# Products of the odd stages that leave out the border's block row

## The reference

```
def basic_block(x, w1, w2, stride=1, ds=None):
    out = relu(conv3(x, w1, stride) * BN_S)          # 3x3, padding 1
    out = conv3(out, w2, 1) * BN_S
    identity = conv1x1(x, ds, stride) * BN_S if ds is not None else x
    return relu(out + identity)

x = basic_block(x, e0b0c1, e0b0c2)                   # 64x64
x = basic_block(x, e0b1c1, e0b1c2)
f0 = x
x = basic_block(x, e1b0c1, e1b0c2, stride=2, ds=e1b0ds)   # 32x32
x = basic_block(x, e1b1c1, e1b1c2)
f1 = x
x = basic_block(x, e2b0c1, e2b0c2, stride=2, ds=e2b0ds)   # 16x16
x = basic_block(x, e2b1c1, e2b1c2)
x = (relu(deconv2(x, dec0w) * BN_S) + f1) * BN_S
x = (relu(deconv2(x, dec1w) * BN_S) + f0) * BN_S     # deconv2: 2x2 kernel, stride 2
```

## Time and profile before

| | |
|---|---|
| median of 3 runs | 89.10 us (89.04 to 89.35) |
| the profiled execution, its device time | 89.06 us |
| its span, first to last instruction | 87.3 us |
| TensorE busy with matmuls | 80.4 us, 92% of the span, 509 records |
| VectorE, ScalarE, GpSimd busy | 56.6, 43.8, 25.6 us |
| mean granted TensorE clock | 0.99 |

### The profile page before, as it was taken

How to read it: one execution, slowest core, us unless ns; L and a number is a source line. 1 busy time by engine, 2 the same in 40 slices (tenths; PEclk the granted TensorE clock), 3 DMA queues, 4 the chain that set the end, 5 groups by cost and what they waited for, 6 DMA issues and landing times.

```text
span 87.3 us, 1464 instructions
## 1 busy us (share of the span) xinstructions
PE 80.4 (92%) x509; PEld 72.0 (83%) x509; DVE 56.6 (65%) x166; ACT 43.8 (50%) x94; POOL 25.6 (29%) x39
## 2 busy tenths in 40 slices
PE   5999999999999999999999999999999999799700
PEld 3777999998778889999988777999999999587500
DVE  5569999799968696522223567999697877213450
ACT  6005214679555047455530239799999996001300
POOL 7200052799960000444452000100289100000330
PEclk9999999999999999999999999999999999999995
DMA  1979930023475106640000000000000000000075
GB/s 27 247 238 274 315 131 0 0 56 108 153 211 204 30 0 173 188 128 0 0 0 0 0 0 4 0 0 0 0 8 0 0 0 0 0 0 8 4 274 207
DMA packets 4183, 6.51 MB, mean 75 GB/s; under 512 B 464, under 2 KB 2128, under 8 KB 4176
## 3 DMA queue, kind: packets, MB, share of 16 engines
q1 hardware_dynamic: 4032, 6.29, 23.5%
q10 hardware_dynamic: 144, 0.13, 0.5%
HBM read 5.37 MB, written 1.05 MB: 74 GB/s over the span
## 4 chain that ended last, share of the span: by engine, by line
PE 91%; DVE 3%; issue 1%; DVEq 0%
PE psum L843 79%; PE psum L870 8%; DVE result L834 2%; PE psum L1023 1%; PE psum L886 1%; PE psum L863 1%; PE psum L1068 1%; PE psum L879 1%; DVE odd L756 0%; DVEq L175 0%; DVE last L754 0%; DVE flat L752 0%; DVE zeros L678 0%; DVEq L833 0%; DVE eps L680 0%
## 5 line engine op out<-in xcount | busy, mean ns | idle before, releaser
L498 POOL TENSOR_TENSOR odd<-relu,odd 128x363 fp32r<-128x363 f32 x12 | 13.6, 1150 | 15.4 <-ACT odd L563 15.4
L843 PE MATMUL psum<-shared,w_e0b0c 128*128 128x364 f32 x72 | 12.5, 331 | 0.0
L773 DVE SCALAR_TENSOR_TENSOR relu<-psum,inside 128x363 f32<-128x363 f32 (+1 forms) x16 | 8.1, 510 | 6.5 <-PE psum L843 5.1
L843 PEld LDWEIGHTS psum<-shared,w_e0b0c 128*128 128x128 f32 x72 | 12.0, 188 | 0.3 <-issue 0.3
L843 PE MATMUL psum<-shared,w_e0b1c 128*128 128x364 f32 x72 | 12.1, 328 | 0.0
L843 PEld LDWEIGHTS psum<-shared,w_e0b1c 128*128 128x128 f32 x72 | 12.0, 188 | 0.1
L843 PE MATMUL psum<-odd,w_e0b0c 128*128 128x512 f32 x48 | 11.6, 400 | 0.0
L843 PE MATMUL psum<-odd,w_e0b1c 128*128 128x512 f32 x48 | 11.6, 400 | 0.0
L843 PEld LDWEIGHTS psum<-odd,w_e0b1c 128*128 128x128 f32 x48 | 9.1, 189 | 2.2
L843 PEld LDWEIGHTS psum<-odd,w_e0b0c 128*128 128x128 f32 x48 | 9.1, 189 | 2.2
L563 ACT ACTIVATE odd<-relu 128x363 fp32r<-128x363 f32 x12 | 6.1, 507 | 7.2 <-DVE relu L773 7.2
(11 more groups left out here) (125 smaller groups left out, 126.2 us busy)
## 6 DMA issues: line engine op xcount, KB each, us to landing
x_sb<-x_in SPq DMA_DIRECT2D x4, 160.0 KB, 3.8
raw<-e0b0c_in SPq DMA_DIRECT2D x2, 256.0 KB, 4.8
raw<-e0b1c_in SPq DMA_DIRECT2D x2, 256.0 KB, 5.0
raw<-e1b1c_in SPq DMA_DIRECT2D x2, 256.0 KB, 3.2
raw<-e2b1c_in SPq DMA_DIRECT2D x2, 256.0 KB, 2.7
raw<-e1b0c_in SPq DMA_DIRECT2D x1, 448.0 KB, 3.7
raw<-e2b0c_in SPq DMA_DIRECT2D x1, 448.0 KB, 3.9
x_sb<-x_in SPq DMA_DIRECT2D x2, 192.0 KB, 4.0
```

The costliest lines, as they stand in the source:

```text
L498: pool.tensor_tensor(split_of(piece, 1), fp32_of(piece), split_of(piece, 0).bitcast(F32), ALU.subtract).then_inc(lo_ready, 1)
L773: last = dve.scalar_tensor_tensor(out=target, in0=sums, scalar=0.0, in1=mask, op0=ALU.max, op1=ALU.mult)
L843: last = pe.matmul(target, w, moving, start=(first and n == 0), stop=(final and n == len(terms) - 1), skip_group_check=skip)
```

## The change

Each product may now carry a pair of columns; the moving run and the PSUM target are then both cut to it. `inside_columns` gives the pair: a piece that holds the top row drops the first pitch - 1 columns where sy is below 1 (below 2 in a down stage), and a piece that holds the bottom row drops the last row (and the run's padding) where sy is 1 (2 in a down stage). The products that carry start or stop stay whole. In odd stages the order of the four shifts is turned (2, 3, 0, 1) where that lets start or stop fall on a whole product. Even stages, sides products, shortcuts and the decoder stay as they are.

```
             def products(target, terms, first=True, final=True, skip=False):
-                for n, (w, moving) in enumerate(terms):
-                    last = pe.matmul(target, w, moving, start=(first and n == 0),
-                                     stop=(final and n == len(terms) - 1), skip_group_check=skip)
+                for n, (w, moving, *columns) in enumerate(terms):
+                    ends = (first and n == 0) or (final and n == len(terms) - 1)
+                    columns = [] if ends else columns
+                    last = pe.matmul(within(target, columns), w, within(moving, columns), start=(first and n == 0),
+                                     stop=(final and n == len(terms) - 1), skip_group_check=skip or len(columns) > 0)
                 return last
+            def within(run, columns):
+                if not columns:
+                    return run
+                span = slice(*columns)
+                return run[:, span] if len(run.shape) == 2 else run[:, :, span]
+            def inside_columns(stage, sy, rows, above, below):
+                pitch = ODD_COLS[0] if stage.level == 0 else PITCH[stage.level]
+                whole = rows * pitch
+                if below and sy == (2 if stage.kind == "down" else 1):
+                    return [0, whole - pitch]
+                if above and sy < (2 if stage.kind == "down" else 1):
+                    return [pitch - 1, whole + 1]
+                return []
...
+                def columns(s):
+                    if stage.kind == "even":
+                        return []
+                    return inside_columns(stage, s // shifts, piece.rows, piece.row == 0,
+                                          piece.row + piece.rows == stage.total)
...
-                    whole = [[moving(half, shifts * sy + sx) for sy, sx in WHOLE] for half in range(2)]
+                    whole = [[(moving(half, shifts * sy + sx), *columns(shifts * sy + sx)) for sy, sx in WHOLE]
+                             for half in range(2)]
...
-                products(target, [(w[:, 0, s], moving(0, s)) for s in range(shifts ** 2)],
+                whole_first = [2, 3, 0, 1] if stage.kind == "odd" and piece.row == 0 else range(4)
+                products(target, [(w[:, 0, s], moving(0, s), *columns(s)) for s in whole_first],
                          first=not started, final=False)
                 wait_w_lo(pe, k)
-                products(target, [(w[:, 1, s], moving(0, s)) for s in range(shifts ** 2)], first=False, final=False)
-                low_terms = [(w[:, 0, s], moving(1, s)) for s in range(shifts ** 2)]
+                products(target, [(w[:, 1, s], moving(0, s), *columns(s)) for s in range(shifts ** 2)],
+                         first=False, final=False)
+                whole_last = [2, 3, 0, 1] if stage.kind == "odd" and piece.row > 0 else range(4)
+                low_terms = [(w[:, 0, s], moving(1, s), *columns(s)) for s in whole_last]
...
             def of_image(image, first):
                 for n in range(EARLY):
-                    pe.matmul(target[:, image], w[:, 0, n], whole[n][:, image], start=(first and n == 0),
-                              stop=False, skip_group_check=True)
+                    columns = [] if n == 0 else columns_2[n]
+                    pe.matmul(within(target[:, image], columns), w[:, 0, n], within(whole[n][:, image], columns),
+                              start=(first and n == 0), stop=False, skip_group_check=True)
...
-            products(target, [(w[:, 0, n], whole[n]) for n in range(EARLY, len(WHOLE))], first=False, final=False,
-                     skip=True)
+            products(target, [(w[:, 0, n], whole[n], *columns_2[n]) for n in range(EARLY, len(WHOLE))], first=False,
+                     final=False, skip=True)
...
-            products(target, [(w_sb[k][:, 0, s], shifted(flat2, s, RUN[2])) for s in range(4)]).then_inc(summed, 1)
+            products(target, [(w_sb[k][:, 0, s], shifted(flat2, s, RUN[2]),
+                               *inside_columns(STAGES[LEVEL2["e2b1c1"].stage], s // 2, ODD_ROWS[2], True, True))
+                              for s in range(4)]).then_inc(summed, 1)
```

More of the change, by code:

```diff
@@ L946, in moving @@
                     return source[:, half, images[0], first:first + run]
+                def columns(s):
[3 more added lines that the diff above has]
+                                          piece.row + piece.rows == stage.total)
                 pe.wait_ge(w_hi, k + 1)
                 if stage.kind == "down":
-                    whole = [[moving(half, shifts * sy + sx) for sy, sx in WHOLE] for half in range(2)]
+                    whole = [[(moving(half, shifts * sy + sx), *columns(shifts * sy + sx)) for sy, sx in WHOLE]
+                             for half in range(2)]
                     wait_source(piece, 0)
                     wait_w_lo(pe, k)
-                    products(target, [(w[:, part, n], m) for part in range(2) for n, m in enumerate(whole[0])],
+                    products(target, [(w[:, part, n], *m) for part in range(2) for n, m in enumerate(whole[0])],
                              final=False)
                     wait_source(piece, 1)
-                    products(target, [(w[:, 0, n], m) for n, m in enumerate(whole[1])], first=False, final=False)
+                    products(target, [(w[:, 0, n], *m) for n, m in enumerate(whole[1])], first=False, final=False)
                     pe.wait_ge(sides_by_act, images[-1] + 1)
@@ L1019, in _ @@
                      for sy, sx in WHOLE]
+            columns_2 = [inside_columns(STAGES[LEVEL2["e2b0c1"].stage], sy, ODD_ROWS[2], True, True) for sy, _ in WHOLE]
             def of_image(image, first):
                 for n in range(EARLY):
-                    pe.matmul(target[:, image], w[:, 0, n], whole[n][:, image], start=(first and n == 0),
-                              stop=False, skip_group_check=True)
+                    columns = [] if n == 0 else columns_2[n]
+                    pe.matmul(within(target[:, image], columns), w[:, 0, n], within(whole[n][:, image], columns),
+                              start=(first and n == 0), stop=False, skip_group_check=True)
             wait_half(pe, source_of_level(2, 0), 0)
```

## The result

The changed kernel takes 87.95 us (median of 4 runs, 87.89 to 88.33) against 89.07 (4 runs, 88.90 to 89.35): a ratio of 0.9889, interval 0.9869 to 0.9909. (The ratio on record isn't the quotient of the two medians, which is 0.9874.) Forecast were 88.1 from 89.10, a gain of 1.0; measured is 1.1. The profiled execution took 87.95 us, its span is 86.1 against 87.3.

What follows compares the result with a forecast made beforehand. TensorE bounds the kernel (92% busy, 91% of the last chain). Of 1.22 us in cut columns, 0.69 + 0.01 + 0.31 = 1.01 arrives: 89.06 - 1.01 = 88.05, forecast 88.1 with the median 0.04 higher; range 87.75 to 88.5.

Steps and rivals of the forecast that it cites:

- The price of a column: TensorE's wide matmuls at levels 0 and 1: 0.44 ns per column cut, from distances between starts, ends 0.43 and 0.48.
- Rival B: TensorE matmuls: columns worth a third, through the load or a cost of cutting the PSUM target; 88.8 us, chance 0.06.
- What is taken back: TensorE's waits behind the cuts: level 0 keeps 0.69 us, e1b0c1 0.01 of 0.21, the rest 0.31; sum 1.01.
- 0.01 of slack before the shortcut's load: Second image's shortcut in e1b0c2 waits for ScalarE's corner copies; only 0.01 us of e1b0c1's saving passes.
- Rival A: e1b0 waits on VectorE's and ScalarE's copies give way, so another 0.20 us arrives; 87.9 us, chance 0.15.
- GpSimd's low half: First image's last piece at level 0: ready for 13.78, TensorE coming at 13.81, just enough; 0.01 us charged.
- the second image's sides: e1b0c1: VectorE's copy plus 0.23 us gives 60.20 against a need at 60.24, so that half passes.
- the second down stage: Sides copies behind ScalarE's skip0 copies could start 0.18 us earlier; e1b1c1 asks for 0.15, so it fits.
- Rival C: First-stage low half, second image's sides and second down stage's sides each miss, costing 0.25 us; 88.35 us, chance 0.10.
- the 0.23 us from producer to matmul: At tight waits, a matmul needs its producer some 0.23 us before: 0.12 to the load, 0.11 more to the matmul.
- The cut of `of_image`: Level 2: cut from 82 to 74 columns costed at nothing, paced by 0.11 us loads; up to 0.03 us if wrong.
- Rival D: Tail from about 75 us: TensorE's clock falls to half, adding 3.3 us; 91.4 us, chance 0.03.

Runs made afterwards that it cites:

- e12: Changed kernel with the 48 cut products of level 0 over 260 columns, output not the reference's; single run, e0b1c1 10.85 us, 0.119 us a cut product.
- e8: Changed kernel with the 48 cut products of level 0 over 200 columns, output not the reference's; single run, e0b1c1 10.63 us, 0.110 us a cut product.
- e1: Changed kernel with the products of e1b0c1 whole again, all other cuts kept; 88.08 us, ratio 0.9875 to the kernel before.
- e6: Changed kernel with ScalarE's skip scaling moved ahead of its sides copies and VectorE's image 0 side copies each one place earlier; 87.58 us, ratio 0.9834.
- e7: Changed kernel with earlier ScalarE skip scaling and earlier VectorE image 0 side copies, but e1b0c1 whole again; 88.09 us, ratio 0.9879.
- e4: Changed kernel with ScalarE's scaling of image 0's skip moved into idle time before its first sides copies; 87.89 us, ratio 0.9867 to the kernel before.
- e5: Changed kernel with VectorE's side copies of image 0 each made one place earlier; 87.99 us, ratio 0.9861 to the kernel before.
- e2: Only the level 0 odd stages cut (48 matmuls, 1584 columns), against the kernel before; 88.42 us, ratio 0.9923.
- e9: The changed kernel once more, unaltered, on another chip; 87.98 us, ratio 0.9891 to the kernel before.

## Why the prediction was right

**The price of a column.** Taken from the shapes of the trace before as 0.44 ns; (11.98 - 11.64)/24/33 = 0.43 in e0b1c1, and e12 gives 0.45 over a hundred columns. Level 0 was forecast to shorten by 0.35 in each stage: 0.34 in e0b1c1 and 0.38 in e0b0c1. Rival B, columns worth less or a cut target that costs, is out by these and by e8 and e12.

**What is taken back.** This was the step that could have gone wrong by 0.20 us: all columns together would have been 1.22. That e1b0c1 brings 0.01 of its 0.21 was read from two small distances, 0.19 in place of 0.135 at the sides and 0.01 of slack before the shortcut's load. e1 shows it from one side, e6 against e7 from the other. Of the two waits the shortcut's is the one that binds: without it (e4) 0.08 arrive, without the other alone (e5) 0.01, without both 0.28. Rival A is out. The 0.01 of slack was right too: with ScalarE's list as it is the change, e1 and e5 all come to 9.49 or 9.50, with three different amounts of work or waiting ahead of the shortcut, and before the change it was 9.51.

**The tight places elsewhere.** GpSimd's low half, the second image's sides and the second down stage were worked out to pass with some hundredths, and all passed: no wait on GpSimd shows, and e1b1c1, e2b0c1 and e2b1c1 gave 0.14, 0.10 and 0.06 of the forecast 0.15, 0.10 and 0.06. Rival C is out. At the low half the margin is used up:

```profile
12.67 0.75 POOL L491 TENSOR_TENSOR shared<-normed,shared 128x288 fp32r<-128x288 f32 x1
...
13.53 0.19 PEld L845 LDWEIGHTS psum<-shared,w_e0b0c 128*128 128x128 f32 x1
...
13.64 0.46 PE L845 MATMUL psum<-shared,w_e0b0c 128*128 128x330 f32 x2
```

The load that waits comes 0.11 us behind GpSimd's end (13.42), later than its place in the row of loads, and the next matmul starts at 13.64, the usual 0.17 behind the one before it. That is the 0.23 us from producer to matmul of the prediction, just met. In e8, with narrower products, a load behind L491 is late and costs 0.25 us. At the second image's sides L711 ends 0.27 us ahead of the matmul in the changed kernel (59.08 and 59.35), the least in any trace, so what less would do there was not put to the test.

**The cut of `of_image`.** Costed at nothing behind the load of 0.11 us. It holds:

```profile
70.43 0.56 PE L1055 MATMUL psum<-planes,w_e2b0c 128*128 128x82 f32 x4
70.98 1.01 PE L845 MATMUL psum<-planes,w_e2b0c 128*128 128x144 f32 x6
71.82 0.56 PE L1055 MATMUL psum<-planes,w_e2b0c 128*128 128x82 f32 x4
72.22 0.77 PE L845 MATMUL psum<-sides,w_e2b0c 128*128 128x164 f32 x4
```

Each image's four records of `of_image`, half of them now cut to 74 columns, take 0.55 and 0.40 us to the next group, before and after. The six records between them take 0.84 instead of 0.94, and this is the whole 0.10.

**The clock.** Rival D did not happen; the fall that it needs stands nowhere in the tail:

```profile
75.00:80.00 5.00, 4.56 (x54) 3.84 (x58) 1.18 (x5) 0.45 (x2) 0.00 (x0) 1.00 0.02 3
```

The granted clock there is 1.00. Since at the start this row missed a spell of half speed, the distances have to say it too: e2b1c2's eight matmuls of 144 columns take 78.07 - 77.01 = 1.06 us, and 79.27 - 78.21 = 1.06 before.

**What the time hides.** The measured gain is 1.12 us and the stages account for 1.04; the other 0.08 is well within the 0.7 us by which the first product's start moves, and is luck as far as can be told. The forecast was 0.15 above the measured median: 0.08 by this, 0.03 because the stages gave 1.04 and not 1.01, 0.03 because the median of before became 89.07 with a fourth run, and 0.01 by rounding. None of it is a step that failed.

## What to carry to other kernels

Price a cut in a saturated engine by the distance between starts of two shapes in the same trace, and look for the floor below which that price ends (here the load, 0.11 us). Then walk along that engine's waits behind the cut: a stretch whose inputs another engine copies, in a list that began before the cut, keeps its length, and the saving inside it is nothing until that list is shortened. Where two such waits follow each other, begin with the later one: it swallows what the first gives (here 0.01 us for the first alone, 0.08 for the later alone, 0.28 for both). A wait of a few hundredths doesn't show as idle time of TensorE; it shows as one distance between matmuls that is too long, right behind a load that came late.

## What the runs showed of the hardware

The first product's start moves by 0.7 us between traces of kernels that are the same up to there (7.84 to 8.57). Two parts of it can be seen: when the first input lands (VectorE waits 0.25 us for it in e6, 0.48 before, 1.03 in e2), and whether the statistics product runs before or after the fillers go from 0.21 to 0.11 us, which decides if its two records take 0.57 us (before) or 0.42 (after). That change of pace comes anywhere from 4.0 us (e6, e9) to 7.1 us (before), with TensorE at work on the same fillers from 1.1 us on in all of them.

Two loads of 128 rows in a row stand at least 0.107 us apart whatever the matmul's width, which makes some 240 columns of fp32r the narrowest that still pays here (an estimate, 0.110/0.45 ns). From the end of a producer on another engine to the weight load that waits for it 0.05 us pass at ScalarE's corners (63.51 to 63.56 in the changed kernel), and 0.11 at VectorE's sides (56.40 to 56.51) and at GpSimd's low half (13.42 to 13.53). The matmul behind the load counts about 0.11 later (13.64).
